# Attention scores as eight more weight columns with a layer's closing steps inside the next dense stage, and a scatter that follows the zero fill by superblock: a four-part graph network on one core

## What is computed

```python
def _gat_layer(x, src, dst, W, a_src, a_dst, b):
    h = (x @ W).reshape(N, H, C)
    alpha_s = jnp.einsum('nhc,hc->nh', h, a_src)
    alpha_d = jnp.einsum('nhc,hc->nh', h, a_dst)
    e = jax.nn.leaky_relu(alpha_s[src] + alpha_d[dst], NEG_SLOPE)
    m = jax.ops.segment_max(e, dst, num_segments=N)
    ex = jnp.exp(e - m[dst])
    den = jax.ops.segment_sum(ex, dst, num_segments=N)
    alpha = ex / (den[dst] + 1e-16)
    out = jax.ops.segment_sum(h[src] * alpha[:, :, None], dst, num_segments=N)
    return out.reshape(N, H * C) + b
for l in range(W.shape[0]):                       # 3 layers
    x = relu(_gat_layer(x, src, dst, W[l], att_src[l], att_dst[l], bias[l]))
```

## Time and profile before

| | |
|---|---|
| median of three runs | 16749.57 us |
| the profiled execution: its own time | 16653.95 us |
| its span, first to last instruction | 16652.1 us |
| granted TensorE clock, mean | 0.593 of 2.4 GHz |
| zero fill and sort, until the scatter begins | 0 to 275 us |
| scatter (POOL) | 275 to 2577 us |
| stage L0 | 653 to 3393 us |
| `in`, the GCN layers and `out` | 6870 to 8031 us |
| `gat0`, `attend0` | 8059 to 10911 us |
| closing steps and `gat1`, `attend1` | 10911 to 13766 us |
| closing steps and `gat2`, `attend2` | 13766 to 16623 us |

### The profile page before, as it was taken

One profiled execution on the slowest core, in us unless ns is written; L12 is line 12 of the kernel. 1 busy time (PEld: TensorE's weight loads), 2 busy tenths in 40 slices (PEclk: granted clock), 3 DMA queues, 4 the chain that ended last, 5 costly groups with the idle time before them and its releaser, 6 DMA issues. The chain is left out here.

```text
span 16652.1 us, 181011 instructions
## 1 busy us (share of the span) xinstructions
PE 6317.3 (38%) x36108; PEld 5357.2 (32%) x36109; DVE 5208.7 (31%) x16216; ACT 4100.0 (25%) x10462; POOL 8151.6 (49%) x8448
## 2 busy tenths in 40 slices
PE   0100005784444434799433333333333333333333
PEld 0000005762332322577432332323223233322332
DVE  6200003422222222322433333343333334333334
ACT  0000005702333333100222222222222222222222
POOL 2777771003555555100355555545555554555554
PEclk7555555586566666699655555555555555555555
DMA  6000002361221112377222222212222222222221
GB/s 210 11 11 9 9 9 63 81 202 34 39 39 38 39 38 39 95 223 222 82 50 50 52 51 51 51 46 51 50 51 51 51 48 49 51 50 52 52 51 46
DMA packets 1157570, 1039.16 MB, mean 62 GB/s; under 512 B 707670, under 2 KB 822582, under 8 KB 1157072
## 3 DMA queue, kind: packets, MB, share of 16 engines
q1 hardware_dynamic: 809536, 614.67, 13.3%
q0 software_dynamic: 265824, 340.03, 10.2%
q10 hardware_dynamic: 81744, 80.28, 1.5%
HBM read 940.04 MB, written 95.72 MB: 62 GB/s over the span
## 5 line engine op out<-in xcount | busy, mean ns | idle before, releaser
L525 POOL DMA_INDIRECT sb_G<-attention_table,sb_NOW x4992 | 4747.6, 951 | 3530.2 <-issue 1460.3
L860 PE MATMUL sums<-sb_G,sb_HOT 128*128 128x100 f32 (+2 forms) x16640 | 3443.1, 394 | 2724.0 <-ACT sb_HOT L651 1248.0
L860 PEld LDWEIGHTS sums<-sb_G,sb_HOT 128*128 128x128 f32 x16640 | 3285.0, 303 | 3012.0 <-issue 2756.1
L525 POOL DMA_INDIRECT sb_G<-feature_table,sb_NOW x1664 | 1573.9, 946 | 1330.8 <-DVE sb_NOW L1432 817.6
L1878 DVE TENSOR_TENSOR sb_ACC<-sb_ACC,sums 128x100 f32 x4992 | 1280.3, 256 | 2825.4 <-issue 1239.5
L582 POOL DMA_INDIRECT edge_counts<-sb_G x1625 | 1734.0, 1067 | 805.8 <-issue 535.3
L1418 DVE TENSOR_TENSOR sb_ACC<-sb_ACC,sums 128x97 f32 (+1 forms) x3328 | 849.9, 255 | 3956.5 <-remote 2447.7
L647 ACT ACTIVATE sb_H<-sb_iota_row,sb_H 128x128 f32<-128x128 f32 x4992 | 1528.7, 389 | 134.3 <-issue 45.5
L647 ACT ACTIVATE sb_HOT<-sb_iota_row,sb_HOT 128x128 f32<-128x128 f32 x3328 | 1015.4, 389 | 2008.8 <-remote 1381.1
L706 ACT ACTIVATE psC<-sb_SB 128x128 f32<-128x128 f32 x156 | 43.8, 281 | 5839.2 <-DVE sb_SB L1831 4863.5
L1037 PE MATMUL psD<-sb_lone,sb_HOT 1*128 1x4 f32 x312 | 90.7, 359 | 2213.3 <-DVE sb_lone L1838 1713.5
(11 more groups left out here) (435 smaller groups left out, 8993.4 us busy)
## 6 DMA issues: line engine op xcount, KB each, us to landing
sb_G<-edge_counts SPq DMA_DIRECT2D x1152, 256.0 KB, 3.3
sb_H<-rel_rows SPq DMA_DIRECT2D x624, 256.0 KB
sb_G<-in_edge_attr_dram SPq DMA_DIRECT2D x1664, 48.0 KB
sb_G<-attention_table,sb_NOW POOLq DMA_INDIRECT x4992
edge_counts<-sb_LW ACTq DMA_DIRECT2D x12, 6272.0 KB, 42.5
sb_EA<-in_edge_attr_dram SPq DMA_DIRECT2D x1664, 16.0 KB
sb_G<-feature_table,sb_NOW POOLq DMA_INDIRECT x1664
edge_counts<-sb_G POOLq DMA_INDIRECT x1625
```

The lines of the kernel that those rows point to most:

```text
L525: pool.indirect_dma_start(to, None, rows, bass.IndirectOffsetOnAxis(ap=index, axis=0)).then_inc(landed, 16)
L860: last = nc.tensor.matmul(bank[:, k // 4, k % 4 * width:(k % 4 + 1) * width], HOT[:, hot, k, :], G[:, slot, k, 0:width], start=True, stop= ...
```

## The change

Three things, none of which changes what is computed.

1. **Scores as weight columns.** `WG` holds each layer's 96 x 96 weight with eight more columns, the weight times `a_src` and times `a_dst` summed by head, made once in the set-up by 12 DVE instructions. The dense stage of a layer multiplies by all 104 columns, and `attend_to` is two copies.
2. **Closing steps in the next dense stage.** For layers 0 and 1 the multiplication by the reciprocal (all heads in one instruction) and the bias are done group by group in `prepare_layer`, three groups ahead; ACT applies the ReLU where it lifts the turned blocks. The last layer keeps its closing steps, and so do the 1e-16 and the reciprocal of each layer.
3. **The scatter follows the fill.** ACT fills the last superblock first, waits for each DMA but one before it issues the next, and counts those that have landed in `cleared`. POOL waits for `slots_ready` and `due_ready`, then ahead of each of the first three landings (`CAREFUL`) for as many superblocks as that landing's rows can reach (`clear`, at least 2), and ahead of the fourth for all 13.

```diff
-            for g in range(NG):
+            for n, g in enumerate([NG - 1] + list(range(NG - 1))):
                 width = WIDE if g < NG - 1 else 2 * P
                 act.dma_start(counts[g, :, 0:NB, 0:width],
-                              zeros[:, 0:width].unsqueeze(1).broadcast_to([P, NB, width])).then_inc(zeroed, 16)
+                              zeros[:, 0:width].unsqueeze(1).broadcast_to([P, NB, width])).then_inc(zeroed[n % 2], 16)
+                if n:
+                    act.wait_ge(zeroed[(n - 1) % 2], 16 * ((n - 1) // 2 + 1))
+                    act.sem_inc(cleared, 1)
+            act.wait_ge(zeroed[(NG - 1) % 2], 16 * ((NG - 1) // 2 + 1))
+            act.sem_inc(cleared, 1)
...
-            pool.wait_ge(zeroed, 16 * NG)
             pool.wait_ge(slots_ready, 1)
+            pool.wait_ge(due_ready, 1)
...
             for n in range(LANDINGS):
+                if n < CAREFUL:
+                    pool.wait_ge(cleared, nc.gpsimd.value_load(clear[0:1, n:n + 1], min_val=2, max_val=NG))
+                    pool.sem_inc(clear_seen, 1)
+                elif n == CAREFUL:
+                    pool.wait_ge(cleared, NG)
                 if n == EARLY:
                     load_windows()
...
+            nc.tensor.matmul(psD[0:1, 3 * P:3 * P + LANDINGS], stat[0:EP, 0, 2:3],
+                             ident[0:EP, ROWS_TOGETHER - 1:EP:ROWS_TOGETHER], start=True, stop=True).then_inc(keys_turned, 1)
...
+            link(v.tensor_scalar(tiles_i[0:EP, 0:1], dst_i[:, EF - 1:EF], wide_bits, None, right))
+            link(v.tensor_copy(stat[0:EP, 0, 2:3], tiles_i[0:EP, 0:1]))
+            link(v.tensor_scalar(stat[0:EP, 0, 2:3], stat[0:EP, 0, 2:3], 2.0, float(NG), ALU.add, ALU.min))
...
+            link(v.tensor_copy(clear[:, :], psD[0:1, 3 * P:3 * P + LANDINGS]))
...
+            for l in range(LAYERS):
+                for n, r in enumerate((R_ASRC, R_ADST)):
+                    weighted = starts[0:D, (2 * l + n) * D:(2 * l + n + 1) * D]
+                    link(v.tensor_tensor(weighted, WG[:, l, 0:D], ROWS[0:D, r + l, :], ALU.mult))
+                    link(v.tensor_reduce(WG[:, l, D + n * HEADS:D + (n + 1) * HEADS],
+                                         weighted.rearrange("p (h c) -> p h c", h=HEADS), AX.X, ALU.add))
...
-                lift(Stage(f"gat{l}"))
+                lift(Stage(f"gat{l}"), ACT.Relu if l else ACT.Copy)
...
-                dense_stage(Stage(f"gat{l}"), W_GAT + l)
+                dense_stage(Stage(f"gat{l}"), WG[:, l, :], WT + HEADS)
...
-                    dve.wait_ge(SEM["taken"], g + score.base["taken"])
-                    v.tensor_copy(ACC[:, part, 0:D], p)
-                    for n, r in enumerate((R_ASRC, R_ADST)):
-                        last = v.tensor_tensor(by_head[n], p, row(r + l).broadcast_to([P, Q, D]), ALU.mult)
-                    last.then_inc(SEM["scored"], 1)
-                    dve.wait_ge(SEM["scored"], g + (score.base["scored"] + 1))
-                    for n, to in enumerate((ACC[:, part, D:WT], DD[:, part, :])):
-                        last = v.tensor_reduce(to, by_head[n].rearrange("p b (h c) -> p b h c", h=HEADS), AX.X, ALU.add)
-                    return last
-                take(score, attend_to)
+                    v.tensor_copy(ACC[:, part, :], p[:, :, 0:WT])
+                    return v.tensor_copy(DD[:, part, :], p[:, :, WT:WT + HEADS])
+
+                def prepare_layer(g):
+                    part = ds(Q * g, Q)
+                    v.tensor_tensor(H[:, part, :].rearrange("p b (h c) -> p b h c", h=HEADS),
+                                    ACC[:, part, 0:D].rearrange("p b (h c) -> p b h c", h=HEADS),
+                                    ACC[:, part, D:WT].unsqueeze(3).broadcast_to([P, Q, HEADS, C]), ALU.mult)\
+                     .then_inc(SEM["hop_step"], 1)
+                    dve.wait_ge(SEM["hop_step"], g + (score.base["hop_step"] + 1))
+                    return v.tensor_tensor(H[:, part, :], H[:, part, :], row(R_GATB + l - 1).broadcast_to([P, Q, D]), ALU.add)
+
+                take(score, attend_to, prepare=prepare_layer if l else None, width=WT + HEADS)
...
-                for h in range(HEADS):
-                    part = ACC[:, :, h * C:(h + 1) * C]
-                    link(v.tensor_tensor(part, part, ACC[:, :, D + h:D + h + 1].broadcast_to([P, NBP, C]), ALU.mult))
-                link(v.tensor_tensor(ACCF, ACCF, over_blocks(row(R_GATB + l)), ALU.add))
-                if l < LAYERS - 1:
-                    link(v.tensor_scalar(H[:, :, :], ACCF, 0.0, None, ALU.max))
```

More of the change, by code:

```diff
@@ L138, in gnn_kernel @@
         due = sb("due", [1, NG - 1], i32)
+        clear = sb("clear", [1, LANDINGS], i32)
         H_flat = H[:, :, :].rearrange("p b d -> p (b d)")
@@ L250, in gnn_kernel @@
                  "virtual_made",
[L251 removed]
+                 "prepared", "staged", "flipped", "lifted", "hid_product", "hid_ready", "made", "taken", "hop_step", "part_step"]
         NAMES += [f"strip_in{n}" for n in range(RING)] + [f"tile_in{n}" for n in range(UN)]
@@ L284, in gnn_kernel @@
             "dense": dense,
-            "scores": dense | {"scored": NG},
+            "scores": dense,
+            "hop_scores": dense | {"hop_step": NG},
             "hop": dense | {"hop_step": 2 * NG},
@@ L297, in gnn_kernel @@
         for l in range(LAYERS):
-            PLAN += [(f"gat{l}", "scores"), (f"attend{l}", "attend")]
+            PLAN += [(f"gat{l}", "hop_scores" if l else "scores"), (f"attend{l}", "attend")]
         STORED = [16] + [16 + 16 * NG * (n + 1) for n in range(LAYERS)]
@@ L383, in _ @@
             sp.dma_start(WTS[:, W_OUT, :], L2_W_out).then_inc(weights_in, 16)
-            sp.dma_start(WTS[:, W_GAT:W_GAT + LAYERS, :], L3_W.rearrange("l a b -> a l b")).then_inc(weights_in, 16)
+            sp.dma_start(WG[:, :, 0:D], L3_W.rearrange("l a b -> a l b")).then_inc(weights_in, 16)
             for r in range(P // DE):
@@ L615, in root, with lift @@
                 nc.scalar.activation(to, of, ACT.Sqrt).then_inc(root_ready, 1)
-            def lift(t):
+            def lift(t, function=ACT.Copy):
                 def copy(g, half):
@@ L622, in copy @@
                     act.wait_ge(SEM["made"], g + (t.base["made"] - 1))
-                    nc.scalar.activation(zT[0:D, half, :], psA[0:D, :], ACT.Copy).then_inc(SEM["lifted"], 1)
+                    nc.scalar.activation(zT[0:D, half, :], psA[0:D, :], function).then_inc(SEM["lifted"], 1)
                 in_pairs(act, copy)
@@ L817, in product @@
                     for q in range(Q):
-                        last = nc.tensor.matmul((psD, psC)[half][:, q * D:(q + 1) * D],
-                                                zT[0:D, half, q * P:(q + 1) * P], WTS[:, w, :], start=True, stop=True)
+                        last = nc.tensor.matmul((psD, psC)[half][:, q * width:(q + 1) * width],
+                                                zT[0:D, half, q * P:(q + 1) * P], w, start=True, stop=True)
                     last.then_inc(SEM["made"], 1)
@@ L1451, in sum_stage, with take @@
                 add_up(t, ROUNDS - 1, UN, UN - 1, width)
-            def take(t, use, banks=(psD, psC), prepare=None):
+            def take(t, use, banks=(psD, psC), prepare=None, width=D):
                 def use_group(g, half):
                     dve.wait_ge(SEM["made"], g + (t.base["made"] + 1))
-                    use(g, banks[half][:, 0:Q * D].rearrange("p (b d) -> p b d", b=Q)).then_inc(SEM["taken"], 1)
+                    use(g, banks[half][:, 0:Q * width].rearrange("p (b d) -> p b d", b=Q)).then_inc(SEM["taken"], 1)
                 def prepare_group(g):
@@ L1912, in _ @@
                 link(v.reciprocal(ACC[:, :, D:WT], ACC[:, :, D:WT]))
-                for h in range(HEADS):
-                    part = ACC[:, :, h * C:(h + 1) * C]
-                    link(v.tensor_tensor(part, part, ACC[:, :, D + h:D + h + 1].broadcast_to([P, NBP, C]), ALU.mult))
-                link(v.tensor_tensor(ACCF, ACCF, over_blocks(row(R_GATB + l)), ALU.add))
-                if l < LAYERS - 1:
-                    link(v.tensor_scalar(H[:, :, :], ACCF, 0.0, None, ALU.max))
+            for h in range(HEADS):
+                part = ACC[:, :, h * C:(h + 1) * C]
+                link(v.tensor_tensor(part, part, ACC[:, :, D + h:D + h + 1].broadcast_to([P, NBP, C]), ALU.mult))
+            link(v.tensor_tensor(ACCF, ACCF, over_blocks(row(R_GATB + LAYERS - 1)), ALU.add))
             v.scalar_tensor_tensor(X[:, :, :], ACCF, 0.0, X[:, :, :], ALU.max, ALU.add).then_inc(result_ready, 1)
```

24 lines of the change are left out of this document (12 added, 12 removed).

## The result

The changed kernel takes 16597.06 us (median of four runs, 16588.78 to 16611.94), the kernel before, on the same chip, 16750.93 us: ratio 0.9909, 95% interval 0.9892 to 0.9927. That is 154 us less; the forecast was 119 less, at 16630 (16597 to 16682). The median stands at the very edge of that range, and two of the four timed runs lie under it.

What follows compares the result with a forecast made beforehand. No engine is busy for half of the span, so a row of stages, each with its own limit, bounds the kernel. 60 - 1 + 14 + 46 = 119 us off the median 16749.57 gives 16630 us, range 16597 to 16682.

Steps and rivals of the forecast that it cites:

- the forecast case: Whole kernel: all parts gain as priced, 119 us less, 16630 us, own bounds 16610 to 16650; chance 0.68.
- Start of the scatter, 60 us: POOL's scatter starts at 210 instead of 275.0; 63 us earlier less 3 for pace beside the fill, bounds 56 to 64.
- L0's end = 0.89a + 0.11b: L0's end moves by 0.89 of the scatter end's shift a plus 0.11 of the L0 start's shift b.
- The windows moved with the scatter: Start of L0: the windows, for which DVE waited 138.72 us, move with the scatter up to 138 us, so a = b.
- `WG`, 1 us: Set-up: twelve DVE instructions delay L0's start by 2 to 7 us, of which 0.11 counts: 1 us lost at most.
- `gat0`, 14 us: First dense stage: DVE's five instructions per group become two copies; 42.0 us becomes 28, a gain of 14.
- `gat1` and `gat2`, 23 us each: Seams between attention layers: 56.2 us become 33, as `out`; gain 23 each, bounds 17 to 28 (28 if PE alone bounds).
- The subtraction from the median: Whole kernel: the 119 us are taken from the median 16749.57, though the profiled execution ran 96 us below it.
- Rival A: Scatter beside the fill: the two streams get in each other's way, gain near 74 us, 16676 us; chance 0.14.
- Rival B: Three dense stages: TensorE's clock stays low, 38 us gained there in place of 60, total 97, 16652 us; chance 0.12.
- Rival C: L0 doesn't end earlier, its fast part being limited by something else: gain 59 us, 16690 us; chance 0.03.
- Rival D: Attention stages: code at other addresses runs worse; 0.76 us per batch eats the gain, 1 us gives 16787; chance 0.03.

Runs made afterwards that it cites:

- scatter_only: The kernel before with only the third part of the change (fill paced and counted, scatter behind it by superblock): ratio 0.9959 to the kernel before.
- before_again: The kernel before, unchanged, profiled a second time: 16606.51 us, ratio 1.0002.
- scores_closing: The kernel before with the first two parts of the change, the scatter still waiting for all 13 fills: ratio 0.9962 to the kernel before.
- one_more: The changed kernel with one more SP instruction (a semaphore increment) ahead of each L0 tile load: 12467.63 us, the kernel before 12617.17 on that chip.
- after_third: The changed kernel, unchanged, run once more on a chip like the first ones: ratio 0.9913 to the kernel before.
- filler: The changed kernel with 64 memsets of 128x8 added on DVE ahead of its wait for the windows: ratio 0.9927 to the kernel before.
- after_again: The changed kernel, unchanged, profiled a second time: 16463.71 us, ratio 0.9916 to the kernel before.

## Why the prediction was right, and where its sizes were off

- **Sign, mechanism and range: right.** 119 us were forecast, 154, 144 and 141 measured on three chips (ratios 0.9909, 0.9916, 0.9913). Three terms were taken too small; the runs show 140.5 us in the parts of the change, and the other 13 of the 154 lie inside the interval of the result (122 to 181 us). That the range holds the result is in part luck: it does so by 0.06 us, the forecast case's own bounds (16610 to 16650) don't hold it, and nothing in the prediction says why the range goes down to 16597.
- **Start of the scatter, 60 us: measured 65** (3391.5 - 3326.6). The 3 us charged for the pace beside the fill were nothing (1.26 us each), nor did the register loads cost anything. Without these two the forecast's own working gives 65, where its upper bound was 64.
- **L0's end = 0.89a + 0.11b: right**, and now tested at three other places. The prediction has "all engines" idle for 41.7 us of a slow group; that is DVE's idle time, POOL scatters in it, and SP, whose loads the others wait for, is slow at its own instructions. The windows moved with the scatter, but with little to spare. DVE's plan was ready at 370.3 instead of 340.8, and it is the third part that does this: 371.6 in scatter_only, 341.6 in before_again. DVE's short instructions run slower there (below). Of the 138 us that it waited for the windows 40 are left. I had written that up to 138 us they move together; the work ahead of that wait grew, which I did not look for.
- **`WG`, 1 us:** L0's first product comes 2.3 us later in scores_closing than in before_again (655.8, 653.5); a ninth of that is nothing.
- **`gat0`, 14 us: measured 17.2.** Taken from `in` at 26.6 and a clock of 0.74; it has 24.5 at 0.83.
- **`gat1` and `gat2`, 23 us each: measured 29.2.** This is the largest step that was mis-sized. I took `out`'s 33 us with one instruction of DVE less, at a clock of 0.66. From the first `prepare_layer` it is 28 us at 0.74 to 0.77, my bound "by PE alone as `in`". PE had 27.42 us of work in `out` and 23.56 in `gat1`, with wider products: the higher clock more than made up for the columns. Why the clock rose as far as it did, no run shows.
- **The subtraction from the median** came out, but not for a reason that I had: the 96 us between profile and median are most likely two chips, which is inferred.
- **Rival A: out.** 60 scatter DMAs went in 75 us beside the fill. The Trainium skill (DMA: Bandwidth & Descriptors, Queues, rings and completion order) has an engine take turns by whole packets; the 3.1 us per scatter DMA worked out from its largest packet did not show, at 1.26 us. The same section gives 9 to 17 descriptors as typical, which the prediction left out: at the fill's 48 ns each that is an estimate of 0.4 to 0.8 us, less than POOL's own 1.26, and this trace agrees with it.
- **Rival B: out.** The clock rose in all three stages. **Rival C: out**, L0 ended earlier. **Rival D: out**, no attention stage moved by 0.76 us per batch (40 us): on one chip the largest shift is 14.2 us, shorter.

## What to carry to other kernels

Before two profiles are set against each other, compare a stage that the change doesn't touch: if it differs by one per cent, take a second profile of the kernel before on the chip of the changed one. Where a stage runs slowly beside another, write the end of both as a sum with weights (0.89a + 0.11b) before pricing an edit. Price a stage that loses one of its two bounding engines from a stage that the other one bounds alone, clock included: `gat1` went from 56.2 us with its closing steps to 28.0, not to the 33 of `out`. What was removed is no measure of the gain: DVE lost 24 us of work in `gat0` and 24 in `gat1` with the closing steps ahead of it, and the gains were 17.5 and 28 us.

## What the runs showed of the hardware

- **Chips differ.** The kernel before took 16750.93, 16607.78, 16610.06, 16685.4, 16592.43 and, on one chip, 12617.17 us. On the three chips where both kernels were timed in rounds, their ratio was 0.9909, 0.9916 and 0.9913. The one fast chip's gathers are no faster, they only follow each other without pauses: in 500 us of `attend0` POOL gathers 399 times there (7000 to 7500 us in one_more) and 301 times in after_third (9000 to 9500), each gather taking 0.94 and 0.95 us, but in after_third POOL waits 79 us for PE's `sums` and 46 for nothing that the profile names, against 2 us. Its attention stages take 2131 to 2138 us instead of 2780 to 2821. What holds the others up there is not shown.
- **Beside POOL's indirect DMAs some engines' instructions come one in 1.40 us**, as a rule, and SP's and the register instructions of ACT are recorded as 0.70 us long. It held SP or ACT, whichever issued L0's loads, and DVE in its straight-line set-up. DVE in the changed kernel beside the scatter:

```profile
312.28 0.15 DVE L1273 TENSOR_TENSOR sb_plan<-sb_tiles_i 49x1 f32<-49x1 int32 x1 [1.25 <-DVE sb_tiles_i L1271]
313.67 0.15 DVE L1275 TENSOR_TENSOR sb_plan<-sb_plan 49x1 f32<-49x1 f32 x1 [1.24 <-DVE sb_plan L1273]
```

They are 1.40 us apart for 0.15 us of work. The kernel before, 30 us into its scatter, had the same two like this:

```profile
303.61 0.15 DVE L1254 TENSOR_TENSOR sb_plan<-sb_tiles_i 49x1 f32<-49x1 int32 x1
303.79 0.15 DVE L1256 TENSOR_TENSOR sb_plan<-sb_plan 49x1 f32<-49x1 f32 x1
```

That is 0.18 us apart, so the scatter alone isn't enough. And the filler's 64 memsets of 0.07 us went from 372.9 to 453.5, the first five of them in 0.60 us and nearly all others 1.40 us apart. ACT's own short loop was not held in any run in which SP issued the loads (8 in 2.44 us above). What decides which engine is held, and why not on the one chip, stays open: the trace shows no releaser that explains these waits, and no run here tried where the instructions come from.
- **The same stage at another clock:** the MLP behind L1 took 49.6 us in before_again and 69.2 in after_again, its code and data unchanged, at the two clocks shown above.
- **SP's issue bounds L0 in its fast part** (4.93 us for eight loads, 5.35 with an instruction more each). A kernel that issued some of these loads from a second engine only once the scatter is over was not tried.
